# Edge attention on one core: row blocks rounded up to one tile of 128 edges instead of two, V's sums added tile by tile, and two of V's eight heads weighted on ScalarE

## The chip, the cores and the metric

One NeuronCore of a Trainium2 chip runs the whole program in one launch. The time is device time in microseconds; the number for a kernel is the median of its runs. Three runs of the kernel before are given, and one more execution was profiled.

## What is computed

A graph attention layer over 4096 nodes with 512 features and 69632 edges, followed by a dense feed-forward part and a mixture of experts. The change lies in the attention alone:

```python
q = (z @ Wq + bq).reshape(L, H, D)          # L = 4096 nodes, H = 8 heads, D = 64
k = (z @ Wk + bk).reshape(L, H, D)
v = (z @ Wv + bv).reshape(L, H, D)
scores = einsum('ehd,ehd->eh', q[row], k[col]) / sqrt(D) + bias     # 69632 edges
m = segment_max(scores, row)
p = exp(scores - m[row])
out = segment_sum(p / segment_sum(p, row)[row] * v[col], row)
```

The rest (layer norms, projections, the feed-forward part with silu, eight experts of which each row takes two) stays as it is.

## The kernel before

**Sorting and projecting.** `sort_and_project` counts the edges of each block of 128 rows (32 blocks), gives every edge a place, and scatters a record per edge (column, row, eight biases) into `records`. A row block's places begin on a multiple of `SPAN = GROUP * 128` edges (lines 459 to 465), so each block is rounded up to `GROUP` tiles of 128 edges. `GROUPS` (line 19) is a bound fixed when the program is built: 69632 / 256 = 272 full groups and 32 more for the rounding are 304, and `TILES` = 608 tiles of 128 edges. `group_block` holds the row block of each group. Meanwhile the projections write q, k and v to HBM; v gets 65 columns a head, the 65th being 1, so that one product sums the weights too (`VHEAD`, `VROW` = 520).

**Attention, how tiles are laid.** `attention` (from line 634) cuts the 608 tiles into 16 ranges of 38 and walks them in 19 turns; a turn takes 2 tiles (`PAIR`) of each range, so 32 tiles (`TURN`). `tile_at` and `group_at` (lines 734 to 738) say which. The loops `key_turns` and `value_turns` (lines 749 to 763) are written for an odd number of turns, with a rolled loop over two turns at a time. TensorE's, VectorE's and ScalarE's bodies run in this rolled loop; GpSimd's queue is written out in full.

**K loop** (`key_turn` on each engine). GpSimd gathers 128 rows of k for a tile with one indirect DMA (line 803) into one of 16 slots of `fetched`, and waits for the product 16 tiles back. TensorE spreads q over the tile's edges: it loads the owner block's number into a register once for two tiles (line 1164) and multiplies the one-hot matrix `hot_t` with that block of q, held in SBUF, into one of four PSUM banks (line 1168). VectorE multiplies with the gathered k (line 886) and sums six or seven heads (line 843), ScalarE the last one or two (line 1044). ScalarE also makes `hot_t` for four tiles at once (lines 1030, 1036) from what TensorE's line 1141 spreads. A running maximum per row range is kept once a turn (lines 852 to 874).

**V loop** (`value_turn` on each engine, turns from last to first). GpSimd gathers 128 rows of v, 520 columns, per tile (line 812), up to 16 tiles ahead; it waits until VectorE has read the slot (`r_scaled`). ScalarE builds a one-hot matrix per tile in two steps: |iota - row| (line 1078), then relu(1 - x) (line 1109), which waits for the product four tiles back. VectorE multiplies the 520 gathered columns with the tile's eight weights, read from PSUM (line 970). TensorE multiplies the one-hot with this, in two halves of 260 columns into two banks, and accumulates over the two tiles of a group (line 1214). Once per group VectorE loads the owner's number into a register (line 955) and adds the two halves into that block's row of `total` in SBUF (line 961, two instructions of 260 columns). At tiles 4, 8 and 12 of a turn it also takes one step of the next turn's scores (`settle`, lines 941, 944 and 948), the first two of which it waits for itself; ScalarE copies for it (lines 1085, 1086) at tile 1 and takes the exponential (line 1091) at tile 18, and TensorE turns the weights (line 1201) at tile 24.

All synchronisation is written by hand. A `Ring` counts how often a step was done; `wait(eng, i, u)` waits for step `u` of turn `i`. In the V loop the order on VectorE is:

```python
for u in range(TURN):
    eng.wait_ge(s_row[u % SLOTS], fetch_count(m, u) + v_from)
    r_tile.wait(eng, m, u - 4)
    nc.vector.tensor_tensor(product[:, u % 4, :] ..., ALU.mult).then_inc(r_scaled.sem(u), 1)
    if u >= GROUP and u % GROUP == GROUP - 1:
        add(m, u // GROUP - 1)
```

## Time and profile before

| | |
|---|---|
| runs | 3536.39, 3532.98, 3523.99 us; median 3532.98 |
| the profiled execution, its own time | 3529.53 us |
| its span in the profile | 3527.8 us, mean granted TensorE clock 0.902 |
| K loop, first to last gather issued | 841.7 to 1608.8 us of the span |
| V loop, 17th to last gather issued | 1639.7 to 2383.2 us |

In the rows further down, a row of a group reads: line, engine, operation, tile written <- tiles read, shapes, count, then busy time in us and the mean ns of one, then the idle time in front of them and what ended it. PE is TensorE's matmul, PEld its weight load, DVE VectorE, ACT ScalarE, POOL GpSimd. An engine with a q (DVEq) is its sequencer: register loads, register arithmetic and semaphore instructions, which aren't counted as busy. `issue` means that the profile shows nothing that was waited for. Consecutive instructions of a kind are merged in a timeline; starts are closer together than durations, because an instruction starts before the one ahead of it has left the pipeline.

### The profile page before, as it was taken

What the parts mean: (1) busy time and instruction counts of PE and PEld (TensorE: products, weight loads), DVE (VectorE), ACT (ScalarE), POOL (GpSimd) and SP (SyncE); (2) the same over time, 40 slices, a digit from 0 to 9 for tenths busy, and PEclk for the clock granted to TensorE, in tenths of its full rate; (3) what the DMA queues carried; (4) which work ended last, traced back from release to release, by engine and by line L of the source; (5) the groups of instructions that cost most, each with busy time, mean ns of one, the idle gap of its engine ahead of it and who ended that gap; (6) DMA issues with size and microseconds to landing.
All of it is one profiled execution on the core that took longest, in us unless ns stands there. A gap on an engine that the chain in (4) does not pass through costs nothing. (4 is left out here: it accounts for less than half of the span.)

```text
span 3527.8 us, 57760 instructions
## 1 busy us (share of the span) xinstructions
PE 2810.0 (80%) x12074; PEld 1806.6 (51%) x12075; DVE 2507.1 (71%) x5087; ACT 1472.7 (42%) x4642; POOL 2197.7 (62%) x2242
## 2 busy tenths in 40 slices
PE   7888888853878888886888888884999997699950
PEld 5555555531333333334665555553888884466630
DVE  6766666634989999999888888885555551577764
ACT  6322222212655655565554544542344442144420
POOL 2477777776777777776777777771222220188866
PEclk9788888876999999998999999996999998799985
DMA  3444444444777777776777777776222223533349
GB/s 104 175 153 157 138 151 159 138 158 124 210 208 210 209 208 206 210 209 187 213 213 213 211 212 213 213 213 212 85 86 86 86 70 119 201 110 113 113 127 314
DMA packets 234986, 594.26 MB, mean 168 GB/s; under 512 B 51889, under 2 KB 60978, under 8 KB 229938
## 3 DMA queue, kind: packets, MB, share of 16 engines
q0 software_dynamic: 127104, 362.93, 36.3%
q1 hardware_dynamic: 103666, 222.27, 17.7%
q10 hardware_dynamic: 4032, 7.34, 0.6%
q14 instruction: 158, 1.29, 0.1%
q8 instruction: 26, 0.43, 0.1%
HBM read 500.22 MB, written 92.15 MB: 168 GB/s over the span
## 5 line engine op out<-in xcount | busy, mean ns | idle before, releaser
L1214 PE MATMUL at_bank<-product,v_hot 128*128 128x260 f32 x2432 | 629.3, 403 | 119.9 <-DVE product L970 110.6
L1168 PE MATMUL at_bank<-wide,hot_t 128*128 x1216 | 611.8, 625 | 127.8 <-ACT hot_t L1036 66.8
L803 POOL DMA_INDIRECT fetched<-t_k,at_index x608 | 583.0, 959 | 192.8 <-issue 134.1
L812 POOL DMA_INDIRECT fetched<-t_v,at_index x608 | 579.1, 953 | 195.2 <-issue 132.3
L348 POOL DMA_INDIRECT records<-staged,address x544 | 533.3, 980 | 265.0 <-issue 164.9
L1214 PEld LDWEIGHTS at_bank<-product,v_hot 128*128 128x128 f32 x2432 | 442.5, 195 | 301.2 <-issue 126.8
L886 DVE TENSOR_TENSOR product<-at_bank,fetched 128x512 f32<-128x512 f32 x608 | 412.6, 680 | 53.0 <-issue 37.1
L970 DVE TENSOR_TENSOR product<-fetched,at_turn 128x520 f32<-128x520 f32 x608 | 404.4, 686 | 61.8 <-DMA fetched<-t_v,at_index 30.1
L1168 PEld LDWEIGHTS at_bank<-wide,hot_t 128*128 128x128 f32 x1216 | 205.4, 193 | 381.7 <-issue 336.1
L617 PE MATMUL qkv_prod<-wide 128*128 128x512 f32 x768 | 378.2, 653 | 0.0
L843 DVE TENSOR_REDUCE raw_score<-product 128x7 f32<-128x448 f32 x608 | 347.1, 573 | 0.0
L1044 ACT ACTIVATE product<-product 128x64 f32<-128x64 f32 x912 | 228.1, 250 | 282.2 <-DVE product L886 281.2
L1109 ACT ACTIVATE v_hot<-at_shared 128x128 f32<-128x128 f32 x608 | 188.1, 309 | 363.2 <-PE at_bank L1214 362.8
L961 DVE TENSOR_TENSOR wide<-at_bank,wide 128x260 f32 x608 | 230.8, 420 | 61.8 <-issue 29.1
L617 PEld LDWEIGHTS qkv_prod<-wide 128*128 128x128 f32 x768 | 158.9, 211 | 193.4 <-issue 193.4
L1396 POOL TENSOR_TENSOR f_base<-f_x 128x512 f32<-128x512 f32 x32 | 41.3, 1291 | 331.0 <-DVE f_x L1445 328.9
L1078 ACT ACTIVATE at_shared<-iota_f,low_neg 128x128 f32<-128x128 f32 x608 | 234.9, 386 | 2.4 <-ACT v_hot L1109 2.1
L598 PE MATMUL ranks<-counts,low_hot_t 128*128 (+1 forms) x1088 | 178.4, 337 | 66.6 <-issue 53.2
L598 PEld LDWEIGHTS ranks<-counts,low_hot_t 128*128 128x128 f32 x1088 | 175.6, 257 | 71.9 <-issue 71.7
L1573 PE MATMUL f_up<-f_zT,f_w 128*128 128x256 f32 x1536 | 189.8, 284 | 0.0
L1573 PE MATMUL f_down<-f_w,f_hT 128*128 128x512 f32 x768 | 185.6, 397 | 2.3 <-issue 2.3
L1573 PEld LDWEIGHTS f_up<-f_zT,f_w 128*128 128x128 f32 x1536 | 185.1, 190 | 2.1 <-ACT f_h L1530 1.3
(294 smaller groups left out, 4253.8 us busy)
## 6 DMA issues: line engine op xcount, KB each, us to landing
row_bc<-in_src SPq DMA_DIRECT2D x34, 1024.0 KB, 4.7
by_slot<-m_y SPq DMA_DIRECT2D x72, 256.0 KB, 2.0
low_bc<-low_row SPq DMA_DIRECT2D x34, 512.0 KB, 5.5
fetched<-t_k,at_index POOLq DMA_INDIRECT x608, 3.7
fetched<-t_v,at_index POOLq DMA_INDIRECT x608, 3.8
records<-staged,address POOLq DMA_INDIRECT x544, 2.1
t_v<-wide SPq DMA_DIRECT2D x32, 260.0 KB
wide<-in_x SPq DMA_DIRECT2D x32, 256.0 KB, 2.9
```

Source lines behind the costliest of these rows:

```text
L348: eng.indirect_dma_start(records, bass.IndirectOffsetOnAxis(address[:, b, u:u + 1], 0), staged[:, b, u, :], None,).then_inc(put[b][u], 16)
L598: nc.tensor.matmul(ranks[b % 2][:, u * BLOCKS:(u + 1) * BLOCKS], low_hot_t[:, b % 2, u * P:(u + 1) * P], counts[:, :, bass.ds(i * 2 * B + ...
L617: last = nc.tensor.matmul(prod[n][:, :], zT[:, c, kc * P:(kc + 1) * P], w[:, n, kc, :], start=(kc == 0), stop=(kc == KC - 1))
L803: eng.indirect_dma_start(fetched[:, n % SLOTS, 0:C], None, k, bass.IndirectOffsetOnAxis(index[:, t:t + 1], 0)).then_inc(s_row[n % SLOTS], 16)
L812: eng.indirect_dma_start(fetched[:, n % SLOTS, :], None, v, bass.IndirectOffsetOnAxis(index[:, t:t + 1], 0)).then_inc(s_row[n % SLOTS], 16)
L843: nc.vector.tensor_reduce(raw[:, b, u % PAIR, u // PAIR, 0:heads], product[:, u % 4, 0:heads * D].rearrange("p (h d) -> p h d", d=D), AX.X ...
L886: nc.vector.tensor_tensor(product[:, u % 4, 0:C], q_edge[u % 4][:, :], fetched[:, u % SLOTS, 0:C], ALU.mult).then_inc(r_product.sem(u), 1)
L970: nc.vector.tensor_tensor(product[:, u % 4, :].rearrange("p (h w) -> p h w", h=HEADS), fetched[:, u % SLOTS, :].rearrange("p (h w) -> p h ...
L1078: nc.scalar.activation(away[:, u % 4, :], iota_f[:, :], ACT.Abs, bias=low_neg[:, bass.ds(back_of(m) * TURN + u, 1)]).then_inc(r_v_away.sem ...
L1168: nc.tensor.matmul(q_edge[u % 4][:, :], hot_t[:, g % 2, u % BATCH * P:(u % BATCH + 1) * P], q_sb[:, bass.ds(at, 1), :].rearrange("p a c -> ...
L1214: last = nc.tensor.matmul(bank[g % 2 * 2 + n][:, 0:HALF], hot[:, u % 4, :], product[:, u % 4, n * HALF:(n + 1) * HALF], start=first, stop= ...
L1573: last = nc.tensor.matmul(out, stationary(a, k), moving(b, k), start=(k == 0 and n == 0), stop=(k == chunks - 1 and n == len(PASSES) - 1))
```

## The change

`GROUP` becomes 1. A row block is rounded up to 128 edges, so `GROUPS` = `TILES` = 544 + 32 = 576, in 16 ranges of 36 tiles and 18 turns; the turn stays at 32 tiles with `PAIR` = 2 written as a number. The row block of every tile is now loaded by itself, on TensorE in the K loop and on VectorE in the V loop. In the V loop each tile's product starts and stops its own sum in one of three two-bank PSUM buffers (`pair`), and VectorE adds it to `total` with one instruction of 2 x 260 columns, two tiles behind (`LAG`). VectorE weights heads 0 to 5 (390 columns); ScalarE weights heads 6 and 7 with two `Copy` instructions of 65 columns each, with a scale per edge from `act_weight`, which it copies out of PSUM once a turn (`keep_weights`). GpSimd, TensorE and the weights' transposes wait for ScalarE's part too.

The diff, cut to its core (what is left out: new tile declarations, the loops rewritten for an even number of turns, renamed PSUM views):

```diff
@@ -14,7 +14,7 @@
 EDGES = 69632
 BLOCKS = NODES // P
 IN_TILES = EDGES // P
-GROUP = 2
+GROUP = 1
 SPAN = GROUP * P
 GROUPS = -(-EDGES // SPAN) + BLOCKS
 TILES = GROUPS * GROUP
...
@@ -25,6 +25,7 @@
 VHEAD = D + 1
 VROW = HEADS * VHEAD
 DVE_HEADS = (HEADS - 1, HEADS - 2)
+V_DVE = HEADS - 2
 MOVES = 32
 PREP_COUNT = 16 * (IN_TILES // MOVES + 1)
...
@@ -634,18 +635,19 @@
 def attention(nc, moved, count, records, group_block, k, v, mixed, wide, s_q_home):
 
     SLOTS = 16
-    PAIR = GROUP
+    PAIR = 2
     TURN = RANGES * PAIR
     TURNS = RANGE_TILES // PAIR
     BATCH = 4
     BATCHES = TURN // BATCH
-    G2 = TURN // GROUP
+    LAG = 2
     CHUNK = PAIR * P
     LANE = RANGE_TILES * P
     BIG = 3.0e38
     HALF = VROW // 2
     PARTS = 8
-    assert TILES == TURN * TURNS and RANGE_TILES == PAIR * TURNS and TURNS % 2 == 1
+    LAST = TURNS - 1
+    assert TILES == TURN * TURNS and RANGE_TILES == PAIR * TURNS and TURNS % 2 == 0 and GROUP == 1
     assert TILES % SLOTS == 0 and TURN % SLOTS == 0
     k_from = count
     v_from = count + 16 * (TILES // SLOTS)
...
@@ -706,9 +709,9 @@
         carry = sb("carry", [1, 2, RANGES, HEADS])
         carried = sb("carried", [P, 2])
         share = sb("share", [P, BLOCKS, HEADS])
-        bank = [part.enter_context(nc.psum_tensor(f"at_bank{n}", [P, C], F32)) for n in range(4)]
-        q_edge = bank
-        low_ps = [part.enter_context(nc.psum_tensor(f"at_low{n}", [P, C], F32)) for n in range(2)]
+        pair = [part.enter_context(nc.psum_tensor(f"at_pair{n}", [P, 2, C], F32)) for n in range(LAG + 1)]
+        q_edge = [pair[n // 2][:, n % 2, :] for n in range(4)]
+        low_ps = [pair[2][:, n, :] for n in range(2)]
         turn_ps = [part.enter_context(nc.psum_tensor(f"at_turn{n}", [P, C], F32)) for n in range(2)]
         score_ps, key_ps = turn_ps
...
@@ -723,9 +726,9 @@
             one(f"a_{n}", 1) for n in ("biased", "turned", "kept", "keyx", "keyed", "keys", "lanes"))
         s_mask, s_lane = sem("a_mask"), sem("a_lane")
         s_chain, s_ends, s_carry, s_carried, s_clear = (sem(f"a_{n}") for n in ("chain", "ends", "carry", "carried", "clear"))
-        r_v_away, r_v_hot, r_scaled, r_tile = (one(f"v_{n}", TURN) for n in ("away", "hot", "scaled", "tile"))
-        r_total = one("v_total", G2)
-        r_back, r_sub, r_exp, r_weight = (one(f"v_{n}", 1) for n in ("back", "sub", "exp", "weight"))
+        r_v_away, r_v_hot, r_scaled, r_act_scaled, r_tile, r_total = (
+            one(f"v_{n}", TURN) for n in ("away", "hot", "scaled", "act_scaled", "tile", "total"))
+        r_back, r_sub, r_exp, r_weight, r_act_weight = (one(f"v_{n}", 1) for n in ("back", "sub", "exp", "weight", "act_weight"))
         s_fix, s_norm, s_share = (sem(f"v_{n}") for n in ("fix", "norm", "share"))
         r_normed = one("v_normed", PARTS)
         r_out = [sem(f"v_out{n}") for n in range(4)]
...
@@ -809,6 +807,7 @@
                     r_product.wait(eng, TURNS - 1, TURN + n - SLOTS)
                 else:
                     r_scaled.wait(eng, m, u - SLOTS)
+                    r_act_scaled.wait(eng, m, u - SLOTS)
                 eng.indirect_dma_start(fetched[:, n % SLOTS, :], None, v,
                                        bass.IndirectOffsetOnAxis(index[:, t:t + 1], 0)).then_inc(s_row[n % SLOTS], 16)
...
@@ -951,37 +950,35 @@
                 settle(0, 0, step)
             eng.wait_ge(s_clear, 2)
 
-            def add(m, g):
-                at = eng.value_load(groups[0:1, bass.ds(group_at(back_of(m), g), 1)], min_val=0, max_val=BLOCKS - 1)
-                r_tile.wait(eng, m, (g + 1) * GROUP - 1)
-                r_total.wait(eng, m, g - 1)
-                to = total[:, bass.ds(at, 1), :].rearrange("p a w -> p (a w)")
-                for n in range(2):
-                    mine = to[:, n * HALF:(n + 1) * HALF]
-                    ins = nc.vector.tensor_tensor(mine, bank[g % 2 * 2 + n][:, 0:HALF], mine, ALU.add)
-                ins.then_inc(r_total.sem(g), 1)
+            def add(m, u):
+                at = eng.value_load(groups[0:1, bass.ds(tile_at(back_of(m), u), 1)], min_val=0, max_val=BLOCKS - 1)
+                r_tile.wait(eng, m, u)
+                r_total.wait(eng, m, u - 1)
+                to = total[:, bass.ds(at, 1), :].rearrange("p a (n w) -> p (a n) w", n=2)
+                nc.vector.tensor_tensor(to, pair[u % 3][:, :, 0:HALF], to, ALU.add).then_inc(r_total.sem(u), 1)
 
             def value_turn(m, b, more):
-                r_weight.wait(eng, m, 0)
+                r_act_weight.wait(eng, m, 0)
                 for u in range(TURN):
                     eng.wait_ge(s_row[u % SLOTS], fetch_count(m, u) + v_from)
                     r_tile.wait(eng, m, u - 4)
                     at = u % PAIR * P + u // PAIR * HEADS
                     nc.vector.tensor_tensor(
-                        product[:, u % 4, :].rearrange("p (h w) -> p h w", h=HEADS),
-                        fetched[:, u % SLOTS, :].rearrange("p (h w) -> p h w", h=HEADS),
-                        turn_ps[b][:, at:at + HEADS].unsqueeze(2).broadcast_to([P, HEADS, VHEAD]), ALU.mult
+                        product[:, u % 4, 0:V_DVE * VHEAD].rearrange("p (h w) -> p h w", h=V_DVE),
+                        fetched[:, u % SLOTS, 0:V_DVE * VHEAD].rearrange("p (h w) -> p h w", h=V_DVE),
+                        turn_ps[b][:, at:at + V_DVE].unsqueeze(2).broadcast_to([P, V_DVE, VHEAD]), ALU.mult
                     ).then_inc(r_scaled.sem(u), 1)
-                    if u >= GROUP and u % GROUP == GROUP - 1:
-                        add(m, u // GROUP - 1)
-                    elif u == GROUP - 1 and not (isinstance(m, int) and m == 0):
-                        add(m - 1, G2 - 1)
+                    if u >= LAG:
+                        add(m, u - LAG)
+                    elif not (isinstance(m, int) and m == 0):
+                        add(m - 1, TURN + u - LAG)
                     if more and u in (4, 8, 12):
                         settle(m + 1, 1 - b, (u - 4) // 4)
 
             value_turns(eng, value_turn)
-            add(last, G2 - 1)
-            r_total.wait(eng, last, G2 - 1)
+            for u in range(TURN - LAG, TURN):
+                add(LAST, u)
+            r_total.wait(eng, LAST, TURN - 1)
 
             st = Steps(eng, s_share)
             by_head = flat_wide.rearrange("p (b h w) -> p b h w", h=HEADS, w=VHEAD)
...
@@ -1096,6 +1093,13 @@
             back_chunk(0)
             exponentials(0, 0)
 
+            def keep_weights(m, b):
+                r_weight.wait(eng, m, 0)
+                by_tile = turn_ps[b][:, 0:CHUNK].rearrange("p (j c h) -> p j c h", j=PAIR, c=RANGES)
+                nc.scalar.copy(act_weight[:, b, :, :, :], by_tile[:, :, :, V_DVE:]).then_inc(r_act_weight.sem(0), 1)
+
+            keep_weights(0, 0)
+
             def value_turn(m, b, more):
                 for u in range(TURN):
                     if u < TURN - 1:
...
@@ -1108,8 +1112,18 @@
                     r_tile.wait(eng, m, u - 4)
                     nc.scalar.activation(hot[:, u % 4, :], away[:, u % 4, :], ACT.Relu, bias=1.0, scale=-1.0
                                          ).then_inc(r_v_hot.sem(u), 1)
+                    if u == 0:
+                        r_act_weight.wait(eng, m, 0)
+                    eng.wait_ge(s_row[u % SLOTS], fetch_count(m, u) + v_from)
+                    for h in range(V_DVE, HEADS):
+                        ins = nc.scalar.activation(product[:, u % 4, h * VHEAD:(h + 1) * VHEAD],
+                                                   fetched[:, u % SLOTS, h * VHEAD:(h + 1) * VHEAD], ACT.Copy,
+                                                   scale=act_weight[:, b, u % PAIR, u // PAIR, h - V_DVE:h - V_DVE + 1])
+                    ins.then_inc(r_act_scaled.sem(u), 1)
                     if more and u == 18:
                         exponentials(m + 1, 1 - b)
+                    if more and u == 28:
+                        keep_weights(m + 1, 1 - b)
 
             value_turns(eng, value_turn)
...
@@ -1160,12 +1174,11 @@
             def key_turn(i, b):
                 for u in range(TURN):
                     g = u // BATCH
-                    if u % GROUP == 0:
-                        at = eng.value_load(groups[0:1, bass.ds(group_at(i, u // GROUP), 1)], min_val=0, max_val=BLOCKS - 1)
+                    at = eng.value_load(groups[0:1, bass.ds(tile_at(i, u), 1)], min_val=0, max_val=BLOCKS - 1)
                     if u % BATCH == 0:
                         r_hot_t.wait(eng, i, g)
                     r_product.wait(eng, i, u - 4)
-                    nc.tensor.matmul(q_edge[u % 4][:, :], hot_t[:, g % 2, u % BATCH * P:(u % BATCH + 1) * P],
+                    nc.tensor.matmul(q_edge[u % 4], hot_t[:, g % 2, u % BATCH * P:(u % BATCH + 1) * P],
                                      q_sb[:, bass.ds(at, 1), :].rearrange("p a c -> p (a c)"),
                                      start=True, stop=True).then_inc(r_edge.sem(u), 1)
                     if u % BATCH == 1 and not (isinstance(i, int) and i == TURNS - 1 and g >= BATCHES - 2):
...
@@ -1197,6 +1210,7 @@
                 r_exp.wait(eng, m, 0)
                 if not (isinstance(m, int) and m == 0):
                     r_scaled.wait(eng, m, -TURN - 1)
+                    r_act_scaled.wait(eng, m, -TURN - 1)
                 for j in range(PAIR):
                     last = nc.tensor.transpose(turn_ps[b][:, j * P:(j + 1) * P], stage_p[:, b, j * P:(j + 1) * P], ident[:, :])
                 last.then_inc(r_weight.sem(0), 1)
...
@@ -1205,14 +1219,16 @@
 
             def value_turn(m, b, more):
                 for u in range(TURN):
-                    g, first, final = u // GROUP, u % GROUP == 0, u % GROUP == GROUP - 1
                     r_v_hot.wait(eng, m, u)
-                    if first:
-                        r_total.wait(eng, m, g - 2)
+                    if u < LAG:
+                        r_total.wait(eng, m, u - LAG)
+                    elif u > LAG:
+                        r_total.wait(eng, m, u - LAG - 1)
                     r_scaled.wait(eng, m, u)
+                    r_act_scaled.wait(eng, m, u)
                     for n in range(2):
-                        last = nc.tensor.matmul(bank[g % 2 * 2 + n][:, 0:HALF], hot[:, u % 4, :],
-                                                product[:, u % 4, n * HALF:(n + 1) * HALF], start=first, stop=final)
+                        last = nc.tensor.matmul(pair[u % 3][:, n, 0:HALF], hot[:, u % 4, :],
+                                                product[:, u % 4, n * HALF:(n + 1) * HALF], start=True, stop=True)
                     last.then_inc(r_tile.sem(u), 1)
                     if more and u == 24:
                         turn_weights(m + 1, 1 - b)
```

## Rows read from the trace of the kernel before

**Rows 1.** The page: busy time of the engines over the whole span.
```profile
PE 2810.0 (80%) x12074; PEld 1806.6 (51%) x12075; DVE 2507.1 (71%) x5087; ACT 1472.7 (42%) x4642; POOL 2197.7 (62%) x2242
```

**Rows 2.** Busy time by stretches: K loop, what lies between, V loop.
```profile
841.70:1610.00 768.30, 630.37 (x1910) 258.41 (x1910) 714.27 (x1340) 462.97 (x2188) 583.04 (x608) 0.97 0.72 208
1610.00:1639.70 29.70, 6.97 (x21) 3.32 (x21) 23.94 (x42) 15.63 (x38) 15.49 (x17) 0.66 0.55 158
1639.70:2390.00 750.30, 630.14 (x2468) 446.90 (x2468) 628.01 (x1270) 379.16 (x1263) 563.66 (x592) 0.97 0.75 211
```

**Rows 3.** By line, the two gathers: ns min/median/max, first and last start.
```profile
L803 POOL DMA_INDIRECT fetched<-t_k,at_index x608: 942/947/2391, 841.7 to 1608.8; - x152
L812 POOL DMA_INDIRECT fetched<-t_v,at_index x608: 942/947/1376, 1610.1 to 2383.2; - x152
```

**Rows 4.** Waits, K window 860 to 1610, then V window 1700 to 2380: total, times, longest.
```profile
POOL fetched L803 <- DVE product L886: 50.9, 167, 0.3
...
POOL fetched L812 <- DVE product L970: 48.1, 158, 0.3
```

**Rows 5.** Timeline of GpSimd at a boundary of two batches of 16 scatters.
```profile
786.35 0.95 POOL L348 DMA_INDIRECT records<-staged,address  x1 [0.30 <-issue]
787.61 0.96 POOL L348 DMA_INDIRECT records<-staged,address  x1 [0.30 <-issue]
788.88 0.96 POOL L348 DMA_INDIRECT records<-staged,address  x1 [0.30 <-ACT staged L378]
```

**Rows 6.** Timeline of VectorE in the V loop, closely packed.
```profile
2007.51 0.75 DVE L961 TENSOR_TENSOR wide<-at_bank,wide 128x260 f32 x2
2008.18 1.29 DVE L970 TENSOR_TENSOR product<-fetched,at_turn 128x520 f32<-128x520 f32 x2
2009.39 0.75 DVE L961 TENSOR_TENSOR wide<-at_bank,wide 128x260 f32 x2
```

**Rows 7.** By line, sequencers' loads of the owner and their register arithmetic.
```profile
L955 DVEq FUSED_REGOPS  x560: 53/190/210, 1639.7 to 2388.2; - x187
L955 DVEq TENSOR_LOAD <-groups x304: 305/311/553, 1639.1 to 2387.9; - x152
...
L1164 PEldq FUSED_REGOPS  x552: 42/151/168, 851.4 to 1611.0; - x184
L1164 PEldq TENSOR_LOAD <-groups x304: 295/302/494, 850.8 to 1610.6; - x152
```

**Rows 8.** Timeline of VectorE in the V loop, where it had caught up.
```profile
2025.69 0.70 DVE L970 TENSOR_TENSOR product<-fetched,at_turn 128x520 f32<-128x520 f32 x1 [0.88 <-DMA fetched<-t_v,at_index]
2026.71 0.76 DVE L961 TENSOR_TENSOR wide<-at_bank,wide 128x260 f32 x2 [0.33 <-issue]
...
2032.42 0.78 DVE L941 TENSOR_TENSOR_SCAN raw_score<-back_apart,raw_score,at_keyx 128x256 f32<-128x256 bf16 x1
...
2037.43 0.52 DVE L944 SCALAR_TENSOR_TENSOR raw_score<-beyond,carried,raw_score 128x256 f32<-128x256 f32 x1
2037.98 0.70 DVE L970 TENSOR_TENSOR product<-fetched,at_turn 128x520 f32<-128x520 f32 x1
...
2042.34 0.41 DVE L948 TENSOR_TENSOR at_shared<-at_shared,raw_score 128x256 f32 x1
```

**Rows 9.** Groups by line: ScalarE's work per tile in V, its 64-column copies in K.
```profile
L1078 ACT ACTIVATE at_shared<-iota_f,low_neg 128x128 f32<-128x128 f32 x604 | 233.4, 386 | 2.4 <-ACT v_hot L1109 2.1
...
L1109 ACT ACTIVATE v_hot<-at_shared 128x128 f32<-128x128 f32 x605 | 187.2, 309 | 363.2 <-PE at_bank L1214 362.8
...
L1044 ACT ACTIVATE product<-product 128x64 f32<-128x64 f32 x912 | 228.1, 250 | 282.2 <-DVE product L886 281.2
```

**Rows 10.** Groups by line: ScalarE's work once a turn in the V loop.
```profile
L1091 ACT ACTIVATE at_shared<-at_shared 128x256 f32 x16 | 6.7, 416 | 0.0
L1086 ACT COPY back_apart<-apart 128x256 bf16 x16 | 6.4, 399 | 0.0
L1085 ACT COPY at_keyx<-ahead 128x256 f32 x16 | 6.2, 388 | 0.0
```

**Rows 11.** Timeline of TensorE: V loop, packed; then K loop, two batches of four tiles.
```profile
2009.01 10.53 PE L1214 MATMUL at_bank<-product,v_hot 128*128 128x260 f32 x44 [0.16 <-DVE product L970]
...
1187.81 1.98 PE L1168 MATMUL at_bank<-wide,hot_t 128*128 x4 [0.39 <-DVE product L886]
1189.63 0.39 PE L1141 MATMUL at_low<-low_t,ident_b 128*128 x4
1189.85 1.94 PE L1168 MATMUL at_bank<-wide,hot_t 128*128 x4
1192.17 1.98 PE L1168 MATMUL at_bank<-wide,hot_t 128*128 x4 [0.39 <-DVE product L886]
```

23 lines of the change are left out of this document (10 added, 13 removed).

## The prediction

> **What bounds the kernel now.** I read the page first: no engine is at its limit over the whole span, GpSimd not either at 62% [rows 1]. So the stages decide, and I cut the span at the first and last gathers [rows 2]. In the K loop VectorE looks like the bound (714 of 768 us), in the V loop TensorE (630 of 750). The reader should not stop there. The gathers by line [rows 3] show a pace: K's 608 issues lie between 841.7 and 1608.8, so 767.1 / 607 = 1.264 us a tile, and V's from the 17th on between 1639.7 and 2383.2, so 743.5 / 591 = 1.258 us. One gather's median is 0.947 us, and the waits' view puts 0.3 us at most before any of them [rows 4]: the same 0.30 us that stands between two scatters that wait for nothing [rows 5]. 0.95 + 0.30 is the pace. So in both loops GpSimd issues without a real stop, and what it issues is the length of the loop; VectorE and TensorE, however busy, follow. A tile costs 1.26 us in each loop, and only a change in the number of tiles, or an engine that needs more than this per tile, moves the time.
>
> **The tiles removed.** 608 tiles become 576. K: 32 x 1.264 = 40.4 us. V: 32 x 1.258 = 40.3 us. Together 80.7 us off, if every other engine still needs under 1.26 us a tile. The scatter of records (544 of them) and everything behind the attention stay.
>
> **GpSimd's second wait.** A gather in V now waits for ScalarE's half too. The nearest row is the first scatter of a batch, which comes behind two waits and a counter: 787.61 to 788.88 is 1.27 us, the step before it 1.26 [rows 5]. So 0 to 0.01 us, 0 to 6 us over 560 gathers. I take 0, as the wait can be handled while the former gather is being issued.
>
> **VectorE in V, its datapath.** Packed, two adds of 260 columns take 2008.18 - 2007.51 = 0.67 us, two products of 520 take 1.21 [rows 6]: 0.335 and 0.605 each, so 1.04 ns a column and 0.065 us fixed. New per tile: 390 columns, 0.47 us, and one add of 520, 0.605 us (before per tile 0.605 + 0.335): 1.08. The steps of the next turn's scores are 0.78, 0.52 and 0.41 us [rows 8], and the sequencer waits for the first two; behind an add and a product they cost some 2 us a turn, 0.06 a tile. 1.14 is under 1.258, so this costs nothing; the cover is the pace of the gathers.
>
> **VectorE in V, its sequencer.** This is the part that I find close. The owner's number is now loaded for every tile. The load itself takes 311 ns and the register arithmetic around it up to 190 ns apiece [rows 7]. What the chain costs shows where VectorE had caught up: a product started at 2025.69, and the add behind it, with nothing but its load and waits between, at 2026.71 [rows 8]: 1.02 us. Then the sequencer must come back to the next product. From below, 0.03 us: line 944, which it waits for, ends at 2037.43 + 0.52, and the product starts at 2037.98 [rows 8]. From above: a packed pair of tiles takes 2009.39 - 2007.51 = 1.88 us [rows 6] with one such chain and three other dispatches, so at most 0.86 / 3 = 0.29 each. A tile needs 1.02 + (0.03 to 0.29) + 0.06, that is 1.11 to 1.37 us. I take 0.15 for the way back, near the middle, as the only row that shows one alone has 0.03 but with its waits already met: 1.23, just under 1.258. Cost 0; from above (1.37 - 1.258) x 576 = +64 us. Up to 16 gathered tiles lie ahead of VectorE, so a stop of 1 us at `settle` doesn't reach GpSimd.
>
> The Trainium skill, page "DMA: Bandwidth & Descriptors", section "Latency and other measured facts", speaks against this edit: it gives a register load (`tensor_load`) a floor of about 600 ns. The trace disagrees, with 311 and 302 ns as medians. By the page the chain would be 0.29 us longer, an estimate from its figure, and VectorE would need about 1.52 us a tile.
>
> **ScalarE in V.** Two copies of 65 columns come to each tile. The nearest row is the copy of 64 columns in K: 250 ns of duration. With 386 and 309 ns for the two steps of the one-hot that is 0.695 + 0.50 = 1.195 us [rows 9], and 416 + 399 + 388 ns once a turn [rows 10] with at most 400 for the new `keep_weights` add 0.05: 1.245, under 1.258 even with durations laid end to end, which overstates them. Cost 0. Its new wait for the gather stands before the next tile's one-hot, in the same queue, and TensorE waits for both; but the data are needed for that tile anyway, and ScalarE's two copies (0.50) end within 0.03 us of VectorE's product (0.47).
>
> **TensorE in V.** Four matmul passes a tile as before; packed, 44 take 10.53 us [rows 11], 0.96 a tile. No sum stays open over two tiles, which costs nothing. Three buffers with the add two tiles behind: tiles 0 and 1 of a turn wait for the add of two tiles back, which comes one chain after their product, 1.02 + 0.61 = 1.6 us; TensorE is done 0.96 later, and VectorE wants the sum only after two more products, 2.5 + 1.0 us. Nothing.
>
> **TensorE in K.** Its owner is loaded per tile now. Four tiles with two loads are packed in 1191.79 - 1187.81 = 3.98 us, and its period is 4.36 there [rows 11]; GpSimd's pace gives it 5.06. Its load and arithmetic (302 + 151 + 42 ns) are 0.89 of VectorE's (311 + 190 + 53) [rows 7], so the chain is 0.91; with 0.15 for the rest and 0.39 for the spread of a batch, 4 x 1.06 + 0.39 = 4.6 us. Cost 0; from above 4 x (1.02 + 0.29) + 0.39 = 5.6, +0.14 a tile, +82 us.
>
> **Small things.** `keep_weights` stands once before the first product of V: +0.4. The last tile is followed by two chains of load and add instead of one: +1.6.
>
> **The sum.** 3529.5 (the profiled execution's own time) - 80.7 + 2.0 = 3450.8. The median of the runs shown is 3.5 us above that execution; I go half way and forecast **3452 us**, 2.3% less. A difference under 0.3% (10.6 us) is about what a measurement of this kernel can't tell from none.
>
> **Rivals.**
> *A. VectorE's sequencer becomes the bound in V.* For it: 1.23 against 1.258 is thin, and 0.15 is a choice. Against: only 0.03 was seen alone. At 1.31 us a tile, +30: 3482; at its end, +64: 3516. Chance 0.18.
> *B. TensorE's sequencer becomes the bound in K,* for the same reason, with more room (4.6 of 5.06). At 1.31 us, +27: 3479. Chance 0.08.
> *C. Slower than before:* the register loads themselves get long. Their longest are 553 and 494 ns [rows 7], 0.24 and 0.19 over the medians; if all were such, because every tile's load now meets ScalarE's and VectorE's traffic on the memory that holds `groups`, VectorE needs 1.23 + 0.24 = 1.47 us (+122) and TensorE (4 x 1.25 + 0.39) / 4 = 1.35 (+50): 3624. It decides when V alone passes 1.42 us a tile (80.7 - 2 + 10.6 = 89 us over 576 tiles, 0.155 each). Against: 311 is the median and 305 the shortest. Chance 0.04. The page named above, with its 600 ns, would lead here.
> *D. The forecast,* GpSimd's pace in both loops: 0.64. The 0.06 left is for what I don't see, either side.
>
> **Range.** 3440 (D with a quiet chip) to 3492 (A or B up to 1.33 us a tile). Above lie the upper part of A and B and all of C. Faster by over 0.3%: A, B, D and most of the rest, 0.94; within: 0.02; slower: 0.04.
>
> **What would show it.** Right: gathers of K and V x576 at 1.26 us; GpSimd's waits still 0.3 us at most; the V loop, from the 17th gather to the last, near 559 x 1.258 = 703 us. VectorE's add should start 1.02 us behind a product that waited, and the next product 0.03 to 0.29 us of sequencer time after that. Wrong: gathers with gaps over 0.3 us ended by VectorE's product in V (A), by K's product behind a late TensorE (B), or by ScalarE's line of the two copies; or loads with a median over 400 ns (C).

## The result and the profile after

The kernel after takes **3489.76 us** (median of 4 runs, 3482.96 to 3490.76), the kernel before 3533.34 (4 runs): ratio 0.9879, 95% interval [0.9864, 0.9894], so 1.2% less time. The forecast was 3452 in a range of 3440 to 3492. The direction is right, and the number lies inside the range, 2.2 us under its upper end; but of the 78.7 us that the sum took off only 39 came. A ratio here compares the undisturbed executions of the two kernels alone, so further down it isn't always that of the two medians given. The profiled execution took 3490.76 us; its span is 3489.1.

From the page of the kernel after: the engines over the span, which say as little as before, and the queue that brings instructions (packets, MB, share of 16 engines; this queue had 158 packets before):

```profile
PE 2810.9 (81%) x11843; PEld 1744.8 (50%) x11844; DVE 2511.8 (72%) x4949; ACT 1689.6 (48%) x5629; POOL 2136.6 (61%) x2178
...
q14 instruction: 218, 1.79, 0.2%
```

By line, the two gathers, then the last starts of the products that follow them (K's, V's):

```profile
L801 POOL DMA_INDIRECT fetched<-t_k,at_index x576: 940/946/2268, 841.8 to 1573.9; - x192
L811 POOL DMA_INDIRECT fetched<-t_v,at_index x576: 940/946/1312, 1575.1 to 2332.0; - x192
L885 DVE TENSOR_TENSOR product<-at_pair,fetched x576: 672/682/693, 853.4 to 1585.5; 128x512 f32<-128x512 f32 x192
L966 DVE TENSOR_TENSOR product<-fetched,at_turn x576: 545/552/563, 1607.8 to 2341.8; 128x390 f32<-128x390 f32 x192
```

Both counts are 576, and a gather still takes 946 ns. But K now runs at 732.1 / 575 = 1.273 us a tile and V at 1.293 (722.6 / 559), where 1.264 and 1.258 were forecast. The stages, cut at the gathers as in [rows 3]; "tail" is from the last gather of V to the end of VectorE's last instruction of the attention, "rest" all that comes behind it. The forecast's 0.4 us for `keep_weights` stands in the step between the loops:

| us | before | forecast | after | after - forecast |
|---|---|---|---|---|
| K, first to last gather | 767.1 | 726.7 | 732.1 | +5.4 |
| last of K to 17th of V | 30.9 | 31.3 | 35.6 | +4.3 |
| V, 17th to last gather | 743.5 | 703.2 | 722.6 | +19.4 |
| tail | 26.6 | 28.2 | 32.7 | +4.5 |
| rest | 1118.0 | 1118.0 | 1124.4 | +6.4 |

So half of what is missing lies in V. The waits of GpSimd, VectorE and ScalarE in the V loop, 1640 to 2330 us of the span (total, times, longest):

```profile
POOL fetched L811 <- issue: 95.3, 312, 0.6
POOL fetched L811 <- DVE product L966: 53.1, 122, 1.7
POOL fetched L811 <- ACT product L1119: 35.1, 102, 1.3
DVE product L966 <- issue: 23.1, 7, 3.7
ACT at_shared L1075 <- issue: 20.7, 9, 3.2
```

VectorE in the same window of the kernel before:

```profile
DVE product L970 <- issue: 23.3, 7, 3.6
```

In [rows 4] no gather waited for over 0.3 us. Now some wait for up to 1.5 us behind VectorE's product (the two longest, of 1.7, have another cause, below): this is what the prediction named as the sign of its rival A. The last two rows of the kernel after show one reason. VectorE stands still seven times for some 3.3 us, with nothing that it waits for. V is written as a loop over two turns, run eight times, so it jumps back seven times, and these are its places. VectorE did so before too. ScalarE's row is new, but not because of its copies: `group1_alone` below has no copies and shows it too (27.6, 7, 4.3). In the kernel before, ScalarE waited for TensorE in V (up to 5.8 us at a time), which may hide such stops.

Timeline of VectorE in the kernel after, across one jump back (start, duration, and in brackets the idle time before it and what ended it), then a packed piece of the same turn:

```profile
1978.94 0.56 DVE L966 TENSOR_TENSOR product<-fetched,at_turn 128x390 f32<-128x390 f32 x1 [3.63 <-issue]
...
1983.21 0.70 DVE L958 TENSOR_TENSOR wide<-at_pair,wide 128x520 f32 x1 [0.79 <-PE at_pair L1230]
...
1986.14 0.70 DVE L958 TENSOR_TENSOR wide<-at_pair,wide 128x520 f32 x1 [0.32 <-issue]
1986.76 0.74 DVE L940 TENSOR_TENSOR_SCAN raw_score<-back_apart,raw_score,at_keyx 128x256 f32<-128x256 bf16 x1
1987.53 0.56 DVE L966 TENSOR_TENSOR product<-fetched,at_turn 128x390 f32<-128x390 f32 x1
1988.54 0.70 DVE L958 TENSOR_TENSOR wide<-at_pair,wide 128x520 f32 x1 [0.44 <-issue]
...
1991.90 0.70 DVE L958 TENSOR_TENSOR wide<-at_pair,wide 128x520 f32 x1
1992.52 0.48 DVE L943 SCALAR_TENSOR_TENSOR raw_score<-beyond,carried,raw_score 128x256 f32<-128x256 f32 x1
1993.03 0.56 DVE L966 TENSOR_TENSOR product<-fetched,at_turn 128x390 f32<-128x390 f32 x1
1994.04 0.70 DVE L958 TENSOR_TENSOR wide<-at_pair,wide 128x520 f32 x1 [0.45 <-issue]
...
2010.31 0.70 DVE L958 TENSOR_TENSOR wide<-at_pair,wide 128x520 f32 x1
2010.92 0.55 DVE L966 TENSOR_TENSOR product<-fetched,at_turn 128x390 f32<-128x390 f32 x1
2011.43 0.70 DVE L958 TENSOR_TENSOR wide<-at_pair,wide 128x520 f32 x1
...
2228.36 0.56 DVE L966 TENSOR_TENSOR product<-fetched,at_turn 128x390 f32<-128x390 f32 x1 [3.39 <-issue]
```

Packed, a tile takes 2011.43 - 2010.31 = 1.12 us. The forecast's 1.23 holds 0.06 for the score steps, so 1.17 is to be set against it: packed, VectorE is faster than forecast. With what lies between it isn't: the jumps at 1978.94 and 2228.36 are three passes of 64 tiles apart, (2228.36 - 1978.94) / 192 = 1.299 us a tile. That is 0.04 over GpSimd's pace of 1.258. Of the 83.1 us of a pass (64 tiles), 64 x 1.12 = 71.7 are tiles, 3.4 the jump (over the seven, the mean step from product to product there is 4.5 us), 2 x 2.6 the steps of the next turn's scores (worked out below), and the last 3 us are mostly sums that come late from TensorE behind the stop, as at 1983.21.

The same stretch on GpSimd's queue in the kernel after:

```profile
1984.65 0.94 POOL L811 DMA_INDIRECT fetched<-t_v,at_index  x1 [0.90 <-DVE product L966]
1986.09 0.94 POOL L811 DMA_INDIRECT fetched<-t_v,at_index  x1 [0.49 <-DVE product L966]
1988.37 0.94 POOL L811 DMA_INDIRECT fetched<-t_v,at_index  x1 [1.33 <-ACT product L1119]
...
2005.66 0.94 POOL L811 DMA_INDIRECT fetched<-t_v,at_index  x1 [1.75 <-DVE product L966]
```

GpSimd is a full 16 tiles ahead here, so each gather starts 0.27 us behind the end of the product 16 tiles back, and the uneven steps behind the jump pass straight through to it. To count this, each gather of V from the 18th on was paired with VectorE's product 16 tiles back. 42 gathers start within 0.35 us of that product's end and over 1.2525 us, the usual step, after the gather before; they lose 16.5 us together (3 gathers and 0.9 us in the kernel before). What is left over the pace, 6.0 us (before 2.4), are GpSimd's own stops: the gather at 2005.66 starts 2.0 us after its product ended, so the releaser in its row isn't what held it. So of the 19.4 us that V is over the forecast, 15.6 are VectorE's. In K the same count gives 3.1 us held, none before. The end at 1988.37 is put down to ScalarE, but VectorE's product had ended last, at 1988.09. That holds for all 42: ScalarE's copies of that tile had ended earlier than VectorE's product each time, and where a gather lost over 0.3 us, over 2 us earlier. So ScalarE's copies held none of them.

At the end of V the last product starts 2341.8 - 2332.0 = 9.8 us behind its gather, where it was 2386.9 - 2383.2 = 3.7 before (last product, last gather): that difference of 6.1 is the tail's whole growth. At the end of K it is 1585.5 - 1573.9 = 11.6 us, against 1616.7 - 1608.8 = 7.9: most of the step between the stages. What is left of the step, from K's last product to V's 17th gather, is 23.9 us for 23.0 before.

### The profile page after: what moved, and what is told of

The parts are those of the page before. It is cut to its first block and busy times, and to the rows that moved or that the text cites. A ratio compares the mean times of both kernels' runs of the same rounds, so it can differ in the third digit from the quotient of the medians.

```text
span 3489.1 us, 61733 instructions
## 1 busy us (share of the span) xinstructions
PE 2810.9 (81%) x11843; PEld 1744.8 (50%) x11844; DVE 2511.8 (72%) x4949; ACT 1689.6 (48%) x5629; POOL 2136.6 (61%) x2178
## 5 line engine op out<-in xcount | busy, mean ns | idle before, releaser
L1230 PE MATMUL at_pair<-product,v_hot 128*128 128x260 f32 x2304 | 640.5, 408 | 94.8 <-DVE wide L958 37.5
L1181 PE MATMUL at_pair<-wide,hot_t 128*128 x1152 | 598.9, 639 | 106.8 <-ACT hot_t L1033 58.1
L811 POOL DMA_INDIRECT fetched<-t_v,at_index x576 | 546.1, 948 | 212.1 <-issue 102.7
L801 POOL DMA_INDIRECT fetched<-t_k,at_index x576 | 553.8, 961 | 186.6 <-issue 124.3
L1230 PEld LDWEIGHTS at_pair<-product,v_hot 128*128 128x128 f32 x2304 | 404.2, 194 | 325.5 <-issue 152.0
L885 DVE TENSOR_TENSOR product<-at_pair,fetched 128x512 f32<-128x512 f32 x576 | 392.9, 684 | 58.6 <-issue 38.9
L958 DVE TENSOR_TENSOR wide<-at_pair,wide 128x520 f32 x576 | 402.7, 699 | 40.5 <-issue 21.2
L1181 PEld LDWEIGHTS at_pair<-wide,hot_t 128*128 128x128 f32 x1152 | 183.8, 193 | 377.3 <-issue 376.6
L966 DVE TENSOR_TENSOR product<-fetched,at_turn 128x390 f32<-128x390 f32 x576 | 318.3, 553 | 25.8 <-issue 23.1
L1119 ACT ACTIVATE product<-fetched,act_weight 128x65 f32<-128x65 f32 x1152 | 330.0, 333 | 0.0
L384 ACT ACTIVATE qkv_root<-qkv_mv,qkv_eps 128x1 f32<-128x1 f32 x64 | 18.8, 294 | 404.0 <-DVE qkv_mv L96 404.0
```

Source lines behind the costliest of these rows:

```text
L801: eng.indirect_dma_start(fetched[:, n % SLOTS, 0:C], None, k, bass.IndirectOffsetOnAxis(index[:, t:t + 1], 0)).then_inc(s_row[n % SLOTS], 16)
L811: eng.indirect_dma_start(fetched[:, n % SLOTS, :], None, v, bass.IndirectOffsetOnAxis(index[:, t:t + 1], 0)).then_inc(s_row[n % SLOTS], 16)
L885: nc.vector.tensor_tensor(product[:, u % 4, 0:C], q_edge[u % 4], fetched[:, u % SLOTS, 0:C], ALU.mult).then_inc(r_product.sem(u), 1)
L958: nc.vector.tensor_tensor(to, pair[u % 3][:, :, 0:HALF], to, ALU.add).then_inc(r_total.sem(u), 1)
L966: nc.vector.tensor_tensor(product[:, u % 4, 0:V_DVE * VHEAD].rearrange("p (h w) -> p h w", h=V_DVE), fetched[:, u % SLOTS, 0:V_DVE * VHEAD ...
L1119: ins = nc.scalar.activation(product[:, u % 4, h * VHEAD:(h + 1) * VHEAD], fetched[:, u % SLOTS, h * VHEAD:(h + 1) * VHEAD], ACT.Copy, sca ...
```

## The experiments

The theory after the result, **S**: in V, VectorE's mean time a tile (packed chain, stops of the jump back, score steps) is over GpSimd's pace, and the stops and score steps are what puts it there. The rivals: the register chain of every tile (the prediction's A; the chain is the load of the owner's number, the arithmetic on it and the waits in front of the add), ScalarE's two copies, or contention of some kind. Some expectations were made before S had this form.

### The two halves of the change

`group1_alone`: one-tile rounding, V's sums per tile, all eight heads on VectorE. `keep_weights` and all waits for ScalarE's part go too (not shown).

```diff
-V_DVE = HEADS - 2
+V_DVE = HEADS
...
-                    for h in range(V_DVE, HEADS):
-                        ins = nc.scalar.activation(product[:, u % 4, h * VHEAD:(h + 1) * VHEAD], ...
```

> The changed kernel with all eight heads back on VectorE: blocks rounded to one tile and sums added per tile, nothing on ScalarE. Theory 1 (VectorE has no room left in V): its datapath needs 0.605 + 0.605 = 1.21 us a tile, over the 1.11 of its sequencer, and the stops and settle steps come on top (13 us in 64 tiles), so about 1.41 us a tile against the changed kernel's 1.31: V about 55 us longer than in the changed kernel, and on a chip like the first one the kernel is slower than before by about 15 us. Theory 2 (ScalarE's copies and its own stops hold V): V shorter than in the changed kernel, by 10 us or more.

`group2_heads`: the kernel before (`GROUP` = 2) with two of V's heads on ScalarE, with `keep_weights` and the waits that belong to them (not shown).

```diff
+V_DVE = HEADS - 2
...
+                    for h in range(V_DVE, HEADS):
+                        ins = nc.scalar.activation(product[:, u % 4, h * VHEAD:(h + 1) * VHEAD], ...
```

> The kernel before with two heads of V's product on ScalarE and nothing else: 608 tiles, sums over two tiles. Theory 1: V already went at GpSimd's pace, so VectorE's 0.13 us a tile saved buy nothing: within 5 us of the kernel before on a chip like the first. Theory 2: ScalarE's longer code now stops at each jump back and the others wait for it: 5 to 15 us slower than before.

Measured, with the kernel before at 3536.15 us: `group1_alone` 3530.7, ratio 0.9989 [0.9978, 1.0001]; `group2_heads` 3534.42, ratio 0.9995 [0.998, 1.001]. By itself neither half gives anything that can be told from none; together they give 1.2%. GpSimd's waits in V of `group1_alone`, and its VectorE, packed:

```profile
POOL fetched L809 <- DVE product L964: 111.4, 187, 3.1
```

```profile
2060.49 0.69 DVE L956 TENSOR_TENSOR wide<-at_pair,wide 128x520 f32 x1
...
2061.44 0.69 DVE L964 TENSOR_TENSOR product<-fetched,at_turn 128x520 f32<-128x520 f32 x1
2062.04 0.69 DVE L956 TENSOR_TENSOR wide<-at_pair,wide 128x520 f32 x1
2062.65 0.68 DVE L964 TENSOR_TENSOR product<-fetched,at_turn 128x520 f32<-128x520 f32 x1
```

A product and an add of 520 columns are 2062.65 - 2061.44 = 1.21 us a tile, and V takes 757.8 us, 1.356 a tile: VectorE holds GpSimd (counted as above, 89 of its gathers are held, for 49.6 us), and V gives back more than the 32 tiles were worth. V is 35 us longer than in the kernel after, where 55 was expected, and the 15 us that the kernel was expected to take beyond the kernel before didn't come. K (733.4) is that of the kernel after. In `group2_heads` V is 744.3 and K 768.0: GpSimd's pace on 608 tiles, as before, so a lighter VectorE buys nothing; none of its gathers is held. The 0.09 us a tile that VectorE gives up (1.21 to 1.12) is what makes the rounding pay: V went from 757.8 to 722.6. From K's last product to V's 17th gather it is 23.2 us without `keep_weights` (`group1_alone`) and 23.9 with it (`group2_heads`).

### What a tile costs: heads and loads

`heads_7_1`, `heads_5_3` (and `heads_7_1_b`, the first once more): another split of V's heads.

```diff
-V_DVE = HEADS - 2
+V_DVE = HEADS - 1
```

```diff
-V_DVE = HEADS - 2
+V_DVE = HEADS - 3
```

> The changed kernel with seven heads on VectorE (455 columns) and one on ScalarE. Theory 1: VectorE's datapath goes from 1.08 to 0.54 + 0.605 = 1.145 us a tile, over the 1.11 that its sequencer allows, so V takes 0.03 to 0.04 us a tile more, 15 to 25 us. Theory 2 (ScalarE): one of its two copies goes, about 0.22 us of its 0.97 a tile, so V gets shorter by 5 to 15 us. Theory 3 (loads): within 5 us.

> The changed kernel with five heads on VectorE (325 columns) and three on ScalarE. Theory 1: the datapath falls to 1.01 us a tile, but the sequencer still needs 1.11, so V stays within 5 us, with ScalarE at about 1.19 a tile just under. Theory 2 (ScalarE holds the loop): 0.22 us more a tile on ScalarE, V longer by 50 us or more. A theory in which VectorE's datapath alone counts: 0.07 a tile less, V shorter by 15 us.

> VectorE weights seven heads in V (455 columns), ScalarE one: VectorE's packed step rises from 1.11 to 1.145 us a tile, ScalarE's falls by 0.25 us. Theory (VectorE's own time sets V where it is over GpSimd's pace): 0.033 us on all 576 tiles, V 722.6 + 17 to 19 = 740 to 742 us, K as before the edit (732 us), time 3507 to 3511 us. Rival (ScalarE's stops with its two copies hold GpSimd and TensorE): V falls to 705 to 715 us, time 3475 to 3483 us.

`loads_halved` (and `loads_halved_b`): the owner is loaded for every second tile, on VectorE in V and, not shown, in the same way on TensorE in K. It leaves out the right owner of some odd tiles and serves for its times alone.

```diff
-                at = eng.value_load(groups[0:1, bass.ds(tile_at(back_of(m), u), 1)], ...
+                if u % 2 == 0:
+                    owner[0] = eng.value_load(groups[0:1, bass.ds(tile_at(back_of(m), u), 1)], ...
+                at = owner[0]
```

> The changed kernel, in which the owner's number is loaded for even tiles only and used for the odd one behind it too, on VectorE in V and on TensorE in K. It leaves out the right owner of those odd tiles whose block differs from that of the tile ahead. Theory 1: VectorE's packed tile falls from 1.11 to the datapath's 1.08, so V by 0.03 x 559 = 17 us at most, and K by nothing, as TensorE was not its bound. Theory 3 (loads are the main cost of the change on both engines): the whole 19 us that V missed come back, and K's 5 too. Theory 2: nothing.

> The owner's number is loaded for every second tile only, on VectorE in V and on TensorE in K; the odd tile of each two is added to, and multiplied with, the owner of the even one, so that part of the lookup is left out. VectorE's packed step falls from 1.11 to 1.08 us a tile (its datapath). Theory (VectorE's time sets V, its sequencer's chain 0.035 us of it a tile): V 722.6 - 0.035 x 576 = 702, so at GpSimd's pace, 702 to 706 us; K, where VectorE's product and not TensorE's load is late, stays at 730 to 733 us; time 3468 to 3472 us. Rival 1 (the stops alone, whatever the rate between them): V stays at 720 us. Rival 2 (TensorE's load chain has a part in K): K falls to 726 us too.

These runs fell on two chips on which every kernel takes a fifth longer (the kernel before 4255.85 and 4184.35 us). VectorE has 32 to 54 waits of over 2.4 us in V there, where the kernel after has 7, and V runs at 1.66 to 1.71 us a tile whatever the edit. The kernel after itself wasn't run on them, so no ratio below shows what an edit does to it. Times: `heads_7_1` 4206.86 (0.9891 [0.9798, 0.9984]), `heads_5_3` 4229.9 (0.9935 [0.9898, 0.9971]), `loads_halved` 4168.35 (0.9825 [0.9732, 0.9918]); on the other chip `heads_7_1_b` 4140.69, `loads_halved_b` 4096.18 (0.9873 [0.9723, 1.0023]). V took 939.4 and 931.8 us with seven heads, 955.1 with five, 942.8 and 926.5 with half the loads: on one chip the edits differ by 16 us at most, and one kernel differs between the two chips by 8 to 16, so the expected times of V were **not settled** by them. What can be read is the packed step. VectorE of `heads_7_1`, `heads_5_3` and `loads_halved`, in this order:

```profile
2569.85 0.69 DVE L958 TENSOR_TENSOR wide<-at_pair,wide 128x520 f32 x1
2570.46 0.62 DVE L966 TENSOR_TENSOR product<-fetched,at_turn 128x455 f32<-128x455 f32 x1
2571.13 0.70 DVE L958 TENSOR_TENSOR wide<-at_pair,wide 128x520 f32 x1
```

```profile
2618.92 0.70 DVE L958 TENSOR_TENSOR wide<-at_pair,wide 128x520 f32 x1
2619.54 0.48 DVE L966 TENSOR_TENSOR product<-fetched,at_turn 128x325 f32<-128x325 f32 x1
2620.04 0.70 DVE L958 TENSOR_TENSOR wide<-at_pair,wide 128x520 f32 x1
```

```profile
2570.93 0.69 DVE L962 TENSOR_TENSOR wide<-at_pair,wide 128x520 f32 x1
2571.54 0.55 DVE L970 TENSOR_TENSOR product<-fetched,at_turn 128x390 f32<-128x390 f32 x1
2572.01 0.69 DVE L962 TENSOR_TENSOR wide<-at_pair,wide 128x520 f32 x1
```

The usual packed step from product to product is 1.143 us for 455 columns, 1.11 for 325 and 1.077 for 390 with half the loads. With 390 and all loads the kernel after has two: 1.115 is its median, and 1.077 stands mostly at the two or three tiles behind the third score step of a turn, which no wait follows, so that the sequencer can get ahead. So 1.077 is the datapath, the 1.08 that the prediction worked out, and 1.11 is the register chain: with 325 columns the datapath needs less, and the usual step stays. Fewer columns than 390 bring next to nothing. The chain costs 0.035 us a tile beyond the datapath, 20 us over 576 tiles if all of it counted.

### The stops and the score steps

`v_unroll_dve`: VectorE's loop over V holds four turns instead of two, the other engines' two.

```diff
-            with eng.Fori(0, (TURNS - 2) // 2) as j:
-                for b in range(2):
-                    body(j * 2 + (b + 1), 1 - b, True)
+            with eng.Fori(0, (TURNS - 2) // per) as j:
+                for n in range(per):
+                    body(j * per + (n + 1), (n + 1) % 2, True)
```

> The changed kernel with one edit: VectorE's V loop is rolled over four turns instead of two, so it jumps back 3 times instead of 7. Theory 1 (VectorE has no room left: 1.11 us a tile packed, plus a stop of 3.3 us at each jump back and the settle steps, makes 84.0 us in turns 7 and 8, 1.31 us a tile, against GpSimd's 1.25): four stops with the disturbed tiles behind them (3.3 + 2.6 us each) go, V from the 17th to the last gather falls from 722.6 us to 705 to 712, the kernel by 12 to 20 us. Theory 2 (ScalarE's new copies and waits hold the loop): ScalarE's own loop is untouched, under 4 us. Theory 3 (the owner's load per tile is the cost): under 4 us too, since the loads stay.

On the first of the two slower chips: 4223.67 us, 0.9936 [0.99, 0.9973], V 951.6. Its stops are hidden among the others there, so the 12 to 20 us expected of it are not settled either.

`unroll_all`: the same with four turns in the loop for TensorE, VectorE and ScalarE, in K and in V.

> The changed kernel with K's and V's loops rolled over four turns on TensorE, VectorE and ScalarE: 3 jumps back instead of 7 in each loop, but twice the code in the loop. If the stops of 3 to 5 us belong to the jump back, four of seven go in each loop: V shorter by 12 to 18 us, K and the step from K to V by 5 to 9. If they belong to the amount of code that has to be brought in per turn, which stays the same, nothing changes (under 4 us).

`settle_late`: VectorE no longer waits for either of the first two score steps right behind it, but two tiles later, still ahead of the step that needs it. (`True` leaves out the wait inside `settle`, not shown.)

```diff
-                        settle(m + 1, 1 - b, (u - 4) // 4)
+                        settle(m + 1, 1 - b, (u - 4) // 4, True)
+                    if more and u in (6, 10):
+                        eng.wait_ge(s_fix, Steps(eng, s_fix, m + 1, 2, (u - 6) // 4 + 1).value())
```

> The changed kernel, in which VectorE's sequencer waits for the first two settle steps two tiles later instead of at once. Theory 1: in each turn the sequencer no longer drains VectorE twice, which is 1.1 us of the 2.7 that the settle steps add over 1.11 us a tile: V shorter by 8 to 18 us. Theory 2: under 3 us.

`unroll_late`: both, and `unroll_late_b`, the same kernel once more.

> Both changes together: the rolled loops of K and V hold four turns on TensorE, VectorE and ScalarE (three jumps back instead of seven in each stage), and VectorE's two waits for its own score steps stand two tiles later. Theory (in V VectorE needs 1.11 us a tile plus the stops of the jump back and the waits of the score steps, and with both cut it stays under GpSimd's 1.258): V, 17th to last gather, 701 to 705 us, K 726 as with the longer loop alone, the step between the stages 29, GpSimd never held for over 0.5 us by VectorE's product; time 3454 to 3460 us. Rival (what the longer loop left in V, 708.6 us, is not VectorE's but the gathers' own or ScalarE's): V stays at 708 and the time at 3462 us.

> The same kernel as unroll_late, once more, in the hope of a chip on which the kernel before takes 3530 and not 4180 us. Theory (VectorE's time a turn, with its stops and waits, sets V): V, 17th to last gather, 701 to 705 us, K 726, the step between the stages 29; time 3454 to 3460 us where the kernel before takes 3530 to 3536. Rival (what the longer loop left in V, 708.6 us, is not VectorE's): V stays at 708 and the time at 3462 us. On a chip like the last one only the ratio can be read: 0.975 to 0.985 by either.

Measured, in us (K, step, V, tail and rest as in the table above):

| | time, ratio to before [95%] | K | step | V | tail | rest |
|---|---|---|---|---|---|---|
| after | 3489.76, 0.9879 [0.9864, 0.9894] | 732.1 | 35.6 | 722.6 | 32.7 | 1124.4 |
| settle_late | 3470.45, 0.9819 [0.9793, 0.9844] | 731.2 | 35.8 | 703.8 | 31.6 | 1125.7 |
| unroll_all | 3461.83, 0.979 [0.9762, 0.9818] | 726.3 | 29.1 | 708.6 | 32.2 | 1121.8 |
| unroll_late_b | 3454.18, 0.9774 [0.9761, 0.9788] | 727.7 | 29.0 | 702.8 | 28.7 | 1124.3 |

`unroll_late` itself fell on the second of the slower chips: 4131.89 us, 0.9815 [0.9708, 0.9921]. There only the ratio can be read, and it lies in the 0.975 to 0.985 expected.

`settle_late` was expected to shorten V by 8 to 18 us and gave 18.8. `unroll_all` and `unroll_late_b` lie where expected. The intervals of these two overlap, so what the later waits add to the longer loop is seen in V of the profiled executions (708.6 and 702.8), not in the time.

The stops first. Waits of VectorE and ScalarE in the V loop of `unroll_all`:

```profile
ACT at_shared L1075 <- issue: 11.4, 3, 4.0
DVE product L966 <- issue: 11.4, 3, 4.0
```

Three stops instead of seven, as many as the loop now jumps back, though the code in it is twice as long: they belong to the jump, not to the amount of code. K, the step behind it and V fell by 5.8, 6.5 and 14.0 us. Whether VectorE's own stop counts or the sums that come late because the other two engines stop as well wasn't separated, since `v_unroll_dve`, the run for it, can't be read.

Then the score steps. In V of `settle_late` VectorE still has all seven stops, and yet V is only 0.6 us over the forecast:

```profile
DVE product L967 <- issue: 23.6, 7, 3.8
```

VectorE in `unroll_late_b`, in the turn behind a jump, to be set against 1986.14 to 1988.54 above:

```profile
1959.36 0.70 DVE L959 TENSOR_TENSOR wide<-at_pair,wide 128x520 f32 x1
1959.98 0.74 DVE L941 TENSOR_TENSOR_SCAN raw_score<-back_apart,raw_score,at_keyx 128x256 f32<-128x256 bf16 x1
1960.64 0.54 DVE L967 TENSOR_TENSOR product<-fetched,at_turn 128x390 f32<-128x390 f32 x1
1961.09 0.69 DVE L959 TENSOR_TENSOR wide<-at_pair,wide 128x520 f32 x1
...
1964.36 0.70 DVE L959 TENSOR_TENSOR wide<-at_pair,wide 128x520 f32 x1
1964.97 0.47 DVE L944 SCALAR_TENSOR_TENSOR raw_score<-beyond,carried,raw_score 128x256 f32<-128x256 f32 x1
1965.37 0.55 DVE L967 TENSOR_TENSOR product<-fetched,at_turn 128x390 f32<-128x390 f32 x1
1965.84 0.69 DVE L959 TENSOR_TENSOR wide<-at_pair,wide 128x520 f32 x1
```

From add to add the tile with the scan takes 1961.09 - 1959.36 = 1.73 us instead of 1988.54 - 1986.14 = 2.40, the one with the second step 1.48, where the kernel after has 2.14 (1991.90 to 1994.04). The steps themselves are as long as they were. What went is the wait in front of the next tile's register chain: while the sequencer waits for the scan, it can't load the next owner, and the add behind is late by the chain. This saves 0.67 + 0.66 = 1.33 us a turn, 21 us over 16 turns, and V fell by 18.8.

Both together make V 702.8 us, K 727.7 and the whole 3454.18, 2.3% under the kernel before and 1.1 points under the kernel after. Gathers, the last products and GpSimd's waits (1640 to 2330 us) of `unroll_late_b`:

```profile
L811 POOL DMA_INDIRECT fetched<-t_v,at_index x576: 942/947/1393, 1572.7 to 2303.3; - x192
L967 DVE TENSOR_TENSOR product<-fetched,at_turn x576: 528/550/562, 1598.8 to 2309.1; 128x390 f32<-128x390 f32 x192
```

```profile
POOL fetched L811 <- ACT product L1122: 33.5, 110, 0.3
POOL fetched L811 <- DVE product L967: 32.9, 108, 0.3
```

No gather of V is held (by the count above 0, and 0.9 us in `settle_late`, 3.6 in `unroll_all`), and the last product follows its gather by 5.8 us instead of 9.8. This is the forecast's case D, reached by two edits that touch neither the tiles' work nor their number. As causes by themselves the rivals fall with it: the register load of every tile, ScalarE's copies and all traffic are still there, and V goes at GpSimd's pace. What is shown is a sum. VectorE was over the pace by 0.04 us a tile; the waits behind the score steps are worth 1.33 / 32 = 0.04, four of seven stops about 4 x 6.4 / 576 = 0.04, so either edit brings V nearly back. The chain's 0.035 is a term of the same sum and would nearly do it too; that is worked out and not measured, as `loads_halved` can't be read for V.

## Why the prediction was right, and where it was off

**Tiles removed** (-80.7): right as a mechanism. With VectorE out of the way K and V take 727.7 and 702.8 us, against 726.7 and 703.2 by the sum. **GpSimd's second wait** (0): right; in V of `unroll_late_b` 110 gathers are put down to ScalarE's copies, with 0.3 us before them like the others. **VectorE's datapath** (1.08): right, 1.077. **Its sequencer** (1.23, of it 0.06 for the score steps): the chain is right; where a product waited for a score step, the add starts 1.01 us behind it (1987.53 to 1988.54), for 1.02 forecast. A packed tile takes 1.11 to 1.12 where 1.17 was forecast, so the way back costs 0.09 us and not 0.15. **ScalarE** (at most 1.245): right as a bound and far off as a size. Its line 1075 starts at 1987.24 and again at 1988.21 where nothing holds it, 0.97 us a tile, because the two copies of 333 ns overlap. **Loads** (case C): medians of 309 and 300 ns with all loads in place, as in [rows 7]; slower was never near. The floor of about 600 ns on the Trainium skill's page "DMA: Bandwidth & Descriptors", section "Latency and other measured facts", isn't one here: the medians are 309 to 312 and 300 to 302 ns in every run, and only on the two slower chips do single loads, at most 44 of an engine's 576, take that long.

**What failed** is the sentence "1.14 is under 1.258, so this costs nothing; the cover is the pace of the gathers", and the same conclusion for the sequencer's 1.23. It sets the cost of a packed tile plus the score steps against GpSimd's pace, and leaves a term out: the stop at each jump back, 3.4 us plus some 3 us of late sums behind it, 0.10 us a tile. It was there to be read in the kernel before (the row above, seven stops of 3.6 us at most), but cost nothing while a packed tile took 1.88 / 2 = 0.94 us [rows 6]: 0.32 us a tile was spare. The change took that to 0.14, and 0.10 for the stops with 0.08 for the score steps is more. **The score steps** were undersized too: "some 2 us a turn" is 2.40 - 1.12 = 1.3 for the scan, 2.14 - 1.12 = 1.0 for line 943 and 1.42 - 1.12 = 0.3 for line 947, 2.6 us in all, 0.08 a tile. "Up to 16 gathered tiles lie ahead of VectorE, so a stop of 1 us at `settle` doesn't reach GpSimd" is true of one stop and false of a mean: a reserve puts off what is over the pace and doesn't absorb it.

So **rival A** is what happened in V by its outcome: VectorE needs about the 1.31 us that it was priced with. The price was 3482 us and the time 3489.76. Its mechanism was not the whole: the chain alone, 1.11, would have stayed under the pace. The range held by a little luck: it was drawn for A or B by itself, with no term for the stops, and K, the step, the tail and the rest each brought 4 to 6 us that no rival priced. **K** was read wrongly for the same reason. That no gather waited over 0.3 us [rows 4] was taken for slack, while in the kernel before VectorE fell behind its gathers from turn to turn (by 4.9 us at the third turn, 15.5 at the seventeenth); a turn in the rolled loop took it 41.2 us for GpSimd's 40.4. After the change it takes 41.6 for most of the loop, and the lag grows to 19.2; at 16 steps of 1.25 us, 20 us, GpSimd is held. Why it takes 0.4 us more is open. The owner's load for every tile on TensorE is one candidate: on the first of the two slower chips K took 889.0 us with half the loads, and 917.9 to 923.7 in the three other kernels there. On a chip of the usual speed this wasn't tried. Fewer jumps cure it in any case.

**Small things** (+2.0): the 1.6 us for a second chain behind the last tile didn't come. From V's last product to the end of the tail it is 22.9 us before, after and in `unroll_late_b`; all 6.1 us by which the tail grew are VectorE's lag. `keep_weights` costs 0.7 to 1.0 us and not 0.4, by the pieces from K's last product to V's 17th gather (23.0 and 23.2 us without it, 23.9 in both kernels with it). The 6.4 us in the **rest**, code that the change doesn't touch, stay unexplained. The rest is 1121.8 to 1125.7 us in all four kernels of the last table and in `group1_alone`, and 1118.0 and 1118.6 in the kernel before and `group2_heads`, each from one execution. In the kernel after 3.6 of the 6.4 us are there at the experts' first gather and 5.9 at their last.

## What to carry to other kernels

When a change takes slack from an engine, compare its mean time over a whole pass of the loop, stops and waits included, with the pace of the engine that leads, not its packed step; and look at how far it lags behind its supplier from turn to turn, since a ring of buffers hides a deficit until it is full. Where an engine is near the pace (here 1.12 us packed for 1.258), two cheap edits come before moving work: a longer body of the rolled loop, and a wait on one's own result put later, nearer to its consumer, above all where a chain of register loads stands behind it. And two halves of a change that give nothing alone can still give all of it together.
